# Twenty-one quads of gathered rows fetched before the node table exists, in a graph-convolution kernel

## The reference, cut to what matters

```
h = jnp.maximum(_layernorm(x, axis=-1), 0.0)
l0, l1 = _fctp_scalar_attr(x0, x1, a, W_l1_0, W_l1_1)      # x0, x1: parts of h; a: node_vec1
h = relu(edge_length_embedded @ W_fc1 / sqrt(N_BASIS)) * RELU_GAIN
w = h @ W_fc2 / sqrt(N_RADIAL)
y0 = l0[edge_src];  y1 = l1[edge_src]                       # one row of 160 numbers for every edge
m0 = w0 * y0 * e0;  m1 = (w1 * y0)[:, :, None] * e1[:, None, :]
m2 = (w2 * e0)[:, :, None] * y1;  m3 = w3 * einsum('eud,ed->eu', y1, e1) * INV_SQRT3
s0..s3 = segment_sum(m0..m3, edge_dst) * inv                # edges are sorted by edge_dst
out = x + self_interaction(h) + 0.5 * (sums @ W_l2) * a / FAN_L2
```

## Time and profile before

| | us |
|---|---|
| median of three runs | 4193.35 (4192.62 to 4194.37) |
| the profiled execution | 4196.62 |
| its span, from first to last instruction | 4192.6 |
| table stage, until the first gather of the main loop starts | 108.3 |
| main loop, first gather to end of the last | 4054 |
| what follows the last gather | 30 |

### The profile page before, as it was taken

The page is one execution under the profiler, slowest core; times in us unless marked ns, Lnnn a source line. Parts: engine busy times, 40 slices in busy tenths (PEclk is TensorE's granted clock), DMA queues, the critical chain, the costliest instruction groups (busy, mean ns, idle before and its releaser), DMA issues.

```text
span 4192.6 us, 56998 instructions
## 1 busy us (share of the span) xinstructions
PE 3633.5 (87%) x17149; PEld 2012.1 (48%) x17149; DVE 2004.2 (48%) x6964; ACT 1013.6 (24%) x2227; POOL 3103.3 (74%) x3265
## 2 busy tenths in 40 slices
PE   5888889898889888898888888888888888888887
PEld 5444445444444444444444444444444444444444
DVE  6444444444444444444444444444444444444443
ACT  5222222222222222222222222222222222222222
POOL 2777777777777777777777777777777777777775
PEclk8778787878787777778777878777878777787878
DMA  6455545555555554555545454545455555555454
GB/s 211 121 136 132 137 129 138 130 137 132 136 133 138 132 135 131 136 135 135 137 131 138 130 137 129 139 130 139 129 136 131 138 132 135 132 138 137 130 139 110
DMA packets 717985, 567.04 MB, mean 135 GB/s; under 512 B 394691, under 2 KB 646098, under 8 KB 717296
## 3 DMA queue, kind: packets, MB, share of 16 engines
q0 software_dynamic: 155008, 265.22, 26.1%
q1 hardware_dynamic: 562240, 297.63, 25.2%
q10 hardware_dynamic: 432, 0.48, 0.0%
HBM read 414.84 MB, written 148.11 MB: 134 GB/s over the span
## 4 chain that ended last, share of the span: by engine, by line
POOL 30%; DMA 27%; PE 19%; issue 13%; DVE 11%; SPq 1%; ACT 0%; DVEq 0%; ACTq 0%; POOLq 0%
POOL R L616 30%; DMA R<-l_table,src 26%; PE bank L762 7%; DVE R L724 7%; PE bank L489 5%; DVE R L721 3%; PE bank L752 3%; PE bank L775 3%; SPq L174 1%; DMA l_table<-ls 0%; PE bank L512 0%; DVE st L214 0%; PE bank L531 0%; PE bank L323 0%; DVE hta L297 0%
## 5 line engine op out<-in xcount | busy, mean ns | idle before, releaser
L616 POOL DMA_INDIRECT R<-l_table,src x3223 | 3072.2, 953 | 992.4 <-issue 787.7
L762 PE MATMUL bank<-w,hs 100*128 100x192 f32 x6446 | 1689.1, 405 | 502.2 <-DVE R L724 496.9
L762 PEld LDWEIGHTS bank<-w,hs 100*128 100x128 f32 x6446 | 1302.5, 233 | 1131.1 <-issue 1080.4
L721 DVE TENSOR_TENSOR R<-bank,R 128x256 f32<-128x256 f32 x1612 | 682.6, 423 | 2077.5 <-DMA R<-l_table,src 1108.1
L724 DVE TENSOR_TENSOR R<-bank,R 128x192 f32<-128x192 f32 x3224 | 985.0, 347 | 0.0
L682 ACT ACTIVATE E<-bank 128x320 f32<-128x320 f32 x806 | 352.6, 438 | 2373.0 <-PE bank L775 2335.7
L775 PE MATMUL bank<-R 128*32 128x320 f32 x6448 | 765.2, 555 | 0.0
L752 PE MATMUL bank<-ea,w1s 10*100 10x512 f32 x1612 | 580.2, 803 | 0.8 <-ACT hs L676 0.8
L676 ACT ACTIVATE hs<-bank 100x512 f32<-100x512 f32 x806 | 437.4, 594 | 400.4 <-PE bank L752 400.4
L489 PE MATMUL bank<-Z,D 128*128 128x448 f32 x784 | 426.1, 700 | 6.9 <-DMA Z<-s_tiles 6.9
L489 PEld LDWEIGHTS bank<-Z,D 128*128 128x128 f32 x784 | 186.2, 251 | 275.7 <-issue 268.5
(11 more groups left out here) (74 smaller groups left out, 532.1 us busy)
## 6 DMA issues: line engine op xcount, KB each, us to landing
s_tiles<-E SPq DMA_DIRECT2D x806, 160.0 KB
R<-l_table,src POOLq DMA_INDIRECT x3223
ea<-in_ea_p SPq DMA_DIRECT2D x403, 96.0 KB
Z<-s_tiles SPq DMA_DIRECT2D x392, 96.0 KB
Z<-s_tiles SPq DMA_DIRECT2D x392, 80.0 KB
Z<-s_tiles SPq DMA_DIRECT2D x392, 48.0 KB
x<-in_xp SPq DMA_DIRECT2D x14, 560.0 KB, 6.7
out<-os SPq DMA_DIRECT2D x98, 80.0 KB
```

What stands on the lines that cost most here:

```text
L616: PL.indirect_dma_start(out=Y[:, g % NB, t, :], out_offset=None, in_=T, in_offset=bass.IndirectOffsetOnAxis(ap=src[:, k:k + 1], axis=0),). ...
L721: V.tensor_tensor(p[:, :, :, 0:64], w[:, :, 0:128].rearrange("p t (s c) -> p t s c", s=2), y[:, :, 0:64].unsqueeze(2).to_broadcast([128, n ...
L762: m = PE.matmul(b[:, o * 192:(o + 1) * 192], hs[:, g % 4, t * 128:(t + 1) * 128], w2[:, :], start=True, stop=True, skip_group_check=True)
```

## The change

Twenty-one quads no longer fetch their rows from the table in the main loop. The rule in `raws` picks them, about 38 quads apart: each is six quads after a point k at which bank 7 is free between two node tiles ((33, 39), (67, 73), ... (759, 765)). Their rows are fetched as raw input rows (160 numbers and `a`, so 161) while the table is built, 84 gathers issued by POOL into a ring of seven quads. The ring lies in memory that the main loop uses for `Z` and `D` (now one tile `ZD`). SP stores each raw quad in the DRAM buffer `W` (`raw_rows`), among the stores of the table; a gather into a used ring slot waits for that store. In the main loop SP loads a raw quad back, into memory of `ls`, six steps before k; DVE takes its statistics, ACT centres it, PE transposes and maps it over four steps of the loop, and ACT scales it into the `Y` buffer of quad k + 6. DVE waits for `s_ro` there instead of for gathers. The node tile's `place` behind it also waits for `s_ro`, since both use bank 7.

POOL no longer centres rows. Every fourth tile is centred by DVE (24 of them), the other 74 by ACT (before: 66 by ACT, 32 by POOL). ACT instead of POOL issues six loads of constants. The pieces of `test` begin at step q = 6 instead of 8.

```diff
+def raws(n_nodes, n_edges):
+    nt, ng = plan(n_nodes, n_edges)
+    ready = due(n_nodes, n_edges)
+    free = [ready[j] + 6 for j in range(nt - 1) if ready[j + 1] - ready[j] >= 8 and ready[j] + 13 < ng]
+    n = min(NRAW, len(free) // 3)
+    return [(free[i * len(free) // n], free[i * len(free) // n] + 6) for i in range(n)]
...
+        SP.dma_start(src_raw[:, :], a["src_raw"]).then_inc(s_sr, 16)
...
-            PL.dma_start(t_, a[n_]).then_inc(s_w1, 16)
+            AC.dma_start(t_, a[n_]).then_inc(s_w1, 16)
...
+        PL.wait_ge(s_sr, 16)
+        for r in range(NR):
+            if r >= NRB:
+                PL.wait_ge(s_rs[r % NRB], 16 * (r // NRB))
+            for t in range(G):
+                k = r * G + t
+                PL.indirect_dma_start(
+                    out=ring[:, r % NRB, t, :], out_offset=None, in_=a["xa"],
+                    in_offset=bass.IndirectOffsetOnAxis(ap=src_raw[:, k:k + 1], axis=0),
+                ).then_inc(s_rg[r % NRB], 16)
...
+        def centre_fourth(q):
+            j = 4 * q + 3
...
+            V.tensor_scalar(H[:, q % 2, 3 * C:4 * C], x[:, j, :], mv[:, j, 0:1], 0.0, ALU.subtract,
+                            ALU.max).then_inc(s_hp, 1)
...
+            centre_fourth(q + 1)
             keep_wide(q)
...
-            if q >= 8:
+            if q >= 6:
                 next(pieces, None)
...
+        def raw_store(r):
+            SP.wait_ge(s_rg[r % NRB], 64 * (r // NRB + 1))
+            SP.dma_start(W[r, :, :], ring[:, r % NRB, :, :].rearrange("p t c -> p (t c)")).then_inc(s_rs[r % NRB], 16)
...
+            while nrs < NR and 4 * nrs + 4 <= 3 * q:
+                raw_store(nrs)
+                nrs += 1
+        for r in range(nrs, NR):
+            raw_store(r)
...
             for g in range(NG):
+                if g in raw_of:
+                    continue
                 for u in pairs(g):
...
+            def load_raw(r):
+                if r >= 2:
+                    SP.wait_ge(s_rh, 4 * (r - 1))
+                    SP.wait_ge(s_ra, r - 1)
+                SP.dma_start(back[:, r % 2, :, :].rearrange("p t c -> p (t c)"), W[r, :, :]).then_inc(s_rl[r % 2], 16)
...
                 for u in pairs(g):
-                    V.wait_ge(s_y[g % NB][u], 32 * (g // NB) + 16 * len(tiles(g, u)))
+                    if g in raw_of:
+                        V.wait_ge(s_ro, 5 * raw_of[g] + 5)
+                    else:
+                        V.wait_ge(s_y[g % NB][u], fetched(g, u))
                     weigh(g, u)
...
+                for r in raw_at(g, -2):
+                    raw_stats(r)
+                for r in raw_at(g, 0):
+                    raw_deviations(r)
```

More of the change, by code:

```diff
@@ L54, in build @@
     ends = reach(n_nodes, n_edges)
-    ready = []
-    for e in ends:
-        ready.append(max(-(-e // G), ready[-1] + 5 if ready else 0))
+    ready = due(n_nodes, n_edges)
+    RAW = raws(n_nodes, n_edges)
+    NR = len(RAW)
+    NRB = 7
+    CR = C + 1
+    raw_of = {g: r for r, (k, g) in enumerate(RAW)}
     NCH = SPAN // 16
@@ L161, in build @@
         s_fs = sem("s_fs")
+        s_sr = sem("s_sr")
+        s_rg = [sem(f"s_rg{b}") for b in range(NRB)]
+        s_rs = [sem(f"s_rs{b}") for b in range(NRB)]
         chain = [0]
@@ L245, in blocks @@
             return range(4 * q, min(4 * q + 4, NT))
-        third = [j for j in range(NT) if j % 3 == 2]
-        others = [j for j in range(NT) if j % 3 != 2]
+        fourth = [j for j in range(NT) if j % 4 == 3]
+        others = [j for j in range(NT) if j % 4 != 3]
         def centre(j):
             q, b = divmod(j, 4)
[L252 to L262, removed]
+            AC.wait_ge(s_nm, j // LC + 1)
+            if q >= 2:
+                AC.wait_ge(s_tp, 2 * q - 2)
+            AC.activation(H[:, q % 2, b * C:(b + 1) * C], x[:, j, :], ACT.Relu, bias=nm[:, j:j + 1]).then_inc(s_hn, 1)
+        def centre_fourth(q):
+            j = 4 * q + 3
+            if j >= NT:
+                return
+            V.wait_ge(s_nm, j // LC + 1)
+            if q >= 2:
+                V.wait_ge(s_tp, 2 * q - 2)
+            V.tensor_scalar(H[:, q % 2, 3 * C:4 * C], x[:, j, :], mv[:, j, 0:1], 0.0, ALU.subtract,
+                            ALU.max).then_inc(s_hp, 1)
         def rows_out(q):
@@ L304, in turn @@
             for j in blocks(q):
-                if j % 3 == 2:
-                    PE.wait_ge(s_hp, third.index(j) + 1)
+                if j % 4 == 3:
+                    PE.wait_ge(s_hp, fourth.index(j) + 1)
                 else:
@@ L444, in build @@
         s_zo = sem("s_zo")
+        s_ro = sem("s_ro")
         s_res = sem("s_res")
@@ L448, in load_tiles @@
         def load_tiles(j):
+            if j == 0:
+                raw_kept(SP)
+                for b in range(3):
+                    SP.wait_ge(s_T[b], 16 * ((NQ + 2 - b) // 3))
             if j >= 2:
@@ L481, in places, with place @@
                                    ALU.is_equal).then_inc(s_D, 1)
-        def place(j):
+        def place(j, g):
+            n = len([r for r, (k, h) in enumerate(RAW) if k + 3 < g])
+            if n:
+                PE.wait_ge(s_ro, 5 * n)
             PE.wait_ge(s_z[j % 2], 48 * NCH * (j // 2 + 1))
@@ L606, in pairs, with fetched, raw_at @@
                 return [u for u in range(2) if tiles(g, u)]
+            def fetched(g, u):
+                return 16 * sum(len(tiles(h, u)) for h in range(g % NB, g + 1, NB) if h not in raw_of)
+            def raw_at(g, d):
+                return [r for r, (k, h) in enumerate(RAW) if k + d == g]
             table_there()
             for g in range(NG):
+                if g in raw_of:
+                    continue
                 for u in pairs(g):
@@ L698, in build @@
                     keep_last(j)
+                for r in raw_at(g, -1):
+                    raw_root(r)
+                    raw_centre(r)
+                for r in raw_at(g, 0):
+                    raw_wide(r)
+                for r in raw_at(g, 1):
+                    raw_fifth(r)
+                for r in raw_at(g, 2):
+                    raw_fore(r)
+                for r in raw_at(g, 3):
+                    raw_rear(r)
             def windows(g):
```

142 lines of the change are left out of this document (135 added, 7 removed).

## The result

The changed kernel takes 4081.47 us (median of 4 runs, 4081.03 to 4086.34) beside 4193.4 us of the kernel before: a ratio of 0.9737, with a 95% interval of 0.9724 to 0.975. Its profiled execution took 4081.77 us, with a span of 4077.8.

The account below looks back on a forecast made before the run. The prediction took POOL's list of gathers to bound the main loop. Span 4192.6 - 105.7 (84 gathers fewer) + 15.3 (later start) = 4102.2 us, forecast time 4103 us, range 4092 to 4124.

Parts of the forecast that it names:

- the 100 to 200 named: Sign in the main loop: DVE's wait for gathers would fall by roughly 100 to 200 us.
- term 1: Main loop: 84 gathers leave POOL's list at 1.258 us each, 105.7 us less, if POOL is never held.
- the sum: Whole kernel's span: 4192.6 - 105.7 + 15.3 = 4102.2 us.
- fourth rival: Main loop: something other than POOL's list holds it; 4208 us or the old time; 0.05 shared with POOL fully held.
- The last sign named: Start and end of the main loop: if the start is right and the end is not, term 1 is wrong.
- Term 2: Start of the main loop: raw gathers and their wait for the first store move it from 108.3 to 123.6, +15.3 us.
- The 8 us taken for the gathers in the full stretch: Table stage, DMA engines full until 44: the first 28 raw gathers delay the table stores by 8 us, to 51.6.
- Transfers not slowed: Table stage: raw gathers slow no load, so the loop starts at 115.6 and the time is 4095 us; chance 0.13.
- POOL held in the loop: Main loop: raw quads delay DVE and so POOL; partly 4143 us, chance 0.05; fully 4355, within another 0.05.
- The change not doing what it says: Main loop: POOL only looks continuous, leaving only the later start; 4208 us or the old time; within a shared 0.05.
- DVE and POOL blocking each other: Table stage: DVE operations wait for whole gathers; 4134 us, or 4117 if half do; chance 0.17.
- third rival: Table stage: DVE and POOL block each other, 31 us more if each DVE operation waits, 4134 us; chance 0.17.

Follow-up runs that it names:

- r4: Kernel before with only its six loads of constants issued by ACT instead of POOL, timed in repeated runs: 4171.40 us, ratio 0.9946.
- r1: Changed kernel with the six loads back on POOL, then one added POOL operation, then the gathers, in repeated runs: 4109.28 us, ratio 0.9796.
- r2: Changed kernel with one added POOL operation first, then the six loads on POOL, then the gathers, in repeated runs: 4086.82 us, ratio 0.9742.
- e1: Kernel before with POOL's 32 centrings moved to DVE and ACT, the six loads still on POOL: 4176.48 us, one execution.
- e9: Changed kernel with ten raw quads instead of 21: 4145.08 us, one execution.
- e10: Changed kernel with no raw quads instead of 21: 4174.61 us, one execution.
- v1: Changed kernel with the three main-loop list loads issued between table stores and the test pieces started at step 8 again: 4071.91 us, ratio 0.9711.
- e6: Changed kernel with the six loads back on POOL, then one added POOL operation, then the gathers: 4114.03 us, one execution.
- e8: Kernel of e1 with one added POOL operation behind the six loads: 4208.32 us, one execution.
- e3: Changed kernel with only the six loads put back on POOL's queue, ahead of the raw gathers: 4083.10 us, one execution.
- e5: Changed kernel with one added POOL operation between the raw gathers and the table gathers: 4090.22 us, one execution.
- e11: Changed kernel with one added POOL operation first, then the six loads on POOL, then the gathers: 4095.12 us, one execution.
- r3: Kernel before with an unused tile of 84 columns shifting the tiles' addresses, in repeated runs: 4198.35 us, ratio 1.0011.
- e7: Kernel before with an unused tile of 84 columns shifting the tiles' addresses: 4206.45 us, one execution.
- r5: Changed kernel with one 512-byte load on POOL, then one added POOL operation, then the gathers: 5211.12 us, kernel before 5215.48 on that chip.
- v2: Kernel of v1 with the first three raw stores put between the loads of x: 5224.63 us, ratio 1.0016 to the kernel before, on the slower chip.

## Why the prediction was wrong

**The reading was right.** POOL's list bounds the loop; 84 gathers less give 105.7 us; the raw work is covered, since no gather of the loop waits over 0.3 us; DVE's wait for gathers fell by 162 us, inside the 100 to 200 named.

**The step that failed is in term 1**, "3,139 gathers of the loop at steps of 1.258 us". I took the step from the earlier trace rows as a property of the instruction and charged the remaining gathers with it. They cost 1.2501, which is 25.1 us less over 3,138 steps. With a start 1.5 us later than priced and a tail 0.7 shorter that makes 24.3, and the miss against the sum is 4102.2 - 4077.8 = 24.4. The cause lies in an edit that I dismissed in one sentence, the six loads that moved from POOL to ACT, counted on ACT alone. r4 prices that edit by itself at 22.8 us, and r1 against r2 shows the condition: plain loads on POOL's queue, arithmetic on POOL (with its MODIFY_POOL_CONFIG) behind them, gathers behind both. The kernel before has all three in that order. The changed kernel also removed the arithmetic, which would have been enough by itself (e1). Why this order makes each gather dearer is open. I did name another pace as a sign, under the fourth rival, but only as a way to lose time, and bounded the duration from neither side. The last sign named, a right start with a wrong end, is the one that came: it points at term 1.

**Term 2 was right, in part by luck.** The start is 125.06 for 123.6. The first table store has landed by 51.3 for 51.6; the raw store lands at 54.0 for 53.1; the table lands at 120.3 with forty raw gathers (e9) for 120. The 8 us taken for the gathers in the full stretch answer to the 7.7 between 43.6 and 51.3; with no raw gather (e10) ACT goes on at 44.13 instead of 51.29, so the gathers themselves make 7.2 of it. Two sizes were off and cancelled or did not count: the centring moved to DVE and ACT costs the table some 2.7 us (e1), if that, for 4, on a path that did not set the start; and the 56 last raw gathers, with steps of 1.258 taken for 1.250, still needed 70.8 us for 70.5, since a few of them were stretched. What I had left out is that the order of SP's queue could be changed: v1 shows that the queue's order, with the lists ahead of the first store, was worth 8.5 us more.

**The rivals.** Transfers not slowed: no, a DMA share of 0.91 in 44 to 60 and a start at 125. POOL held in the loop: no, 0.3 us is the longest gap. The change not doing what it says: no, the loop shrank by its full share. DVE and POOL blocking each other is in the trace, at a small price. The source view of DVE's 24 centrings in the changed kernel:

```profile
L313 DVE TENSOR_SCALAR H<-x,mv x24: 286/296/473, 9.4 to 110.7; 128x160 f32<-128x160 f32 x24
```

They take 0.296 us at the median, 0.473 at most, beside gathers of 0.946, so none waited for a whole gather. The other way round there is a block. Two operations of DVE, then the raw gathers that start while these run:

```profile
81.38 0.98 DVE L428 TENSOR_TENSOR rel<-R 128x804 f32<-128x804 int32 x1
...
92.12 0.30 DVE L313 TENSOR_SCALAR H<-x,mv 128x160 f32<-128x160 f32 x1
```
```profile
81.83 1.35 POOL L244 DMA_INDIRECT ZD<-in_xa,src_raw  x1 [0.30 <-issue]
...
92.23 1.00 POOL L244 DMA_INDIRECT ZD<-in_xa,src_raw  x1 [0.30 <-issue]
```

Both gathers end 0.82 us after the end of the DVE operation, and so do the three others of the 84 that are stretched beside DVE (0.81 to 0.82). Each stands until that operation is done and then takes the rest of its usual 0.946 us. Two of the five met a centring, three a piece of the test or of the weights with both inputs in memory. All five together cost 0.8 us, the two behind centrings 0.1, where the third rival had 31: its mechanism is there in part, but only a gather that starts in the wrong moment meets it, and four gathers that start within 0.06 us of a centring's start are not stretched. The rule in the Trainium skill ("SBUF — State Buffer", section "SBUF: two separate sides"), that whichever of the two starts first keeps the shared ports and the other is blocked, agrees with the trace for these five gathers, not for the four; in the other direction this trace shows no DVE operation that waited for a whole gather.

**The range** ended at 4092 because it had no case in which the gather itself got cheaper.

## What to carry to other kernels

Where one engine's list of equal instructions is the bound, the price of one is the largest term of the sum: 8 ns on 3,139 came to 25.1 us, more than the 15.3 that I had worked out for the start of the loop. Look at minimum and median of that instruction in both traces before anything else, and give its price a bound on either side wherever a change alters what that engine does before its list begins. If POOL issues thousands of indirect gathers, issue plain loads from another queue, or put POOL's first arithmetic ahead of them.

## What the hardware showed that I had not expected

- The order of a few instructions in the first 10 us sets the duration of every gather in the next 4 ms: a median of 946 ns (949 in some executions), or 953 (957 in some) with loads, then arithmetic and its MODIFY_POOL_CONFIG, then gathers (r1, e6, e8, the kernel before). Why is open. The state does not come from loads alone (e3), arithmetic alone (e4), arithmetic before loads (r2), or arithmetic alone behind the raw gathers (e5, one execution).
- Executions of equal programs on different chips differ by 2 to 3 ns a gather (r2 1.2504 and e11 1.2528 us, r1 1.2574 and e6 1.2601, r3 1.2578 and e7 1.2603), worth up to 9 us here. Whether the chip or the execution sets it is open; e10 and e9, on one chip, have 1.2501 and 1.2528.
- A gather that starts while DVE is in the middle of an operation with both inputs in memory stands until that is done: 0.40 us more for one gather in the changed kernel, 0.77 in e9. Behind a centring it was 0.06 at most in the changed kernel.
- On one chip the kernel before took 5215 us. The two kernels profiled there, r5 and v2, had POOL held by DVE, and versions with the 84 gathers fewer, worth over 2% elsewhere, stood at 0.9999 and 1.0016.
